# A four-part transformer block: the router splits nine weight pieces instead of 27, and the second attention's first batch is put in another order

## The reference, cut to what matters

```python
x = x + tanh(g_xattn[0]) * L0_xattn(layernorm(x), ctx, ctx, ...)   # 16 heads of 16, rotary positions
x = x + tanh(g_ffn[0])   * L0_ffn(layernorm(x), ...)               # 8 experts, top 2 of each token, and a shared expert
x = x + tanh(g_xattn[1]) * L1_xattn(layernorm(x), ctx, ctx, mask, ...)  # 16 heads of 64, masked softmax
x = x + tanh(g_ffn[1])   * L1_ffn(layernorm(x), ...)               # quantised gate/up/down

def L0_ffn(x):                                   # T = 4096 tokens
    scores = softmax(x @ gate_w.T);  _, indices = top_k(scores + gate_bias, 2)
    combine = sum_k one_hot(indices, 8) * take(scores, indices)
    y = sum_e mlp(x, w1[e], w2[e], w3[e]) * combine[:, e:e+1]
    return y + mlp(x, sw1, sw2, sw3)             # mlp: (silu(x @ w1.T) * (x @ w3.T)) @ w2.T, inner width 512
def L1_xattn(Q, K, V, mask):
    q, k, v = Q @ W_q + b_q, K @ W_k + b_k, V @ W_v + b_v         # inner width 1024
    s = where(mask == 0, -1e9, q k^T / 8);  return softmax(s) v @ W_o + b_o
```

## Time and profile before

| | |
|---|---|
| median of 3 runs | 2144.2 us (2143.4 to 2144.92) |
| the profiled execution | 2143.76 us, its span 2141.7 us |
| TensorE busy | 1743.6 us, 81% of the span |
| VectorE busy | 1415.4 us, 66% |
| ScalarE busy | 1103.9 us, 52% |
| GpSimd busy | 1034.0 us, 48% |
| granted TensorE clock, mean | 0.931 of full speed |

### The profile page before, as it was taken

How to read it: one execution, slowest core, us unless ns; L and a number is a source line. 1 busy time by engine, 2 the same in 40 slices (tenths; PEclk the granted TensorE clock), 3 DMA queues, 4 the chain that set the end, 5 groups by cost and what they waited for, 6 DMA issues and landing times. The chain is left out here.

```text
span 2141.7 us, 45574 instructions
## 1 busy us (share of the span) xinstructions
PE 1743.6 (81%) x14369; PEld 1163.1 (54%) x14375; DVE 1415.4 (66%) x2938; ACT 1103.9 (52%) x2568; POOL 1034.0 (48%) x1543
## 2 busy tenths in 40 slices
PE   0588888886258979999995899999999999998376
PEld 0344444443234546666663676767676767776123
DVE  4356667675975434444444787778787877877796
ACT  1266666664632212222221666666666666666776
POOL 1555555550735732232315666666666666554004
PEclk9689999998569999999997999999999999999697
DMA  3000000000820011222213222222232332320102
GB/s 104 12 9 12 10 10 10 10 5 1 267 78 1 1 47 57 69 71 63 79 44 94 70 73 70 69 72 69 74 78 69 78 77 70 79 63 11 41 1 79
DMA packets 89345, 117.62 MB, mean 55 GB/s; under 512 B 16520, under 2 KB 58768, under 8 KB 89232
## 3 DMA queue, kind: packets, MB, share of 16 engines
q1 hardware_dynamic: 76176, 90.08, 15.6%
q0 software_dynamic: 6528, 17.83, 3.0%
q10 hardware_dynamic: 6528, 8.39, 1.2%
HBM read 56.36 MB, written 17.83 MB: 35 GB/s over the span
## 5 line engine op out<-in xcount | busy, mean ns | idle before, releaser
L1069 POOL TENSOR_SCALAR a_P<-a_P,a_RS 128x256 f32<-128x256 f32 x512 | 254.5, 497 | 235.4 <-DVE a_RS L1351 206.1
L1238 ACT ACTIVATE a_P<-a_pS,a_NM 128x256 f32<-128x256 f32 x512 | 237.9, 471 | 198.3 <-DVE a_NM L1347 194.6
L815 DVE TENSOR_REDUCE a_M<-a_pS 128x2 f32<-128x512 f32 x256 | 164.6, 685 | 142.6 <-PE a_pS L626 142.3
L1247 ACT ACTIVATE a_PH<-a_pT 128x512 f16<-128x512 f32 x256 | 154.1, 602 | 80.5 <-PE a_pT L1163 70.5
L1347 DVE TENSOR_REDUCE a_NM<-a_pS 128x2 f32<-128x512 f32 x256 | 174.7, 682 | 26.3 <-PE a_pS L1155 20.7
L1357 DVE TENSOR_TENSOR a_PL<-a_pT,a_PH 128x512 f16<-128x512 f32 x256 | 172.5, 674 | 16.9 <-ACT a_PH L1247 16.8
L754 ACT ACTIVATE a_PT<-a_pT 128x512 f32<-128x512 f32 x256 | 139.0, 597 | 71.4 <-PE a_pT L645 71.1
L1163 PE MATMUL a_pT<-g_ident,a_P 128*128 128x128 f32 x1024 | 155.9, 275 | 19.9 <-POOL a_P L1069 19.9
L1163 PEld LDWEIGHTS a_pT<-g_ident,a_P 128*128 128x128 f32 x1024 | 120.0, 141 | 38.2 <-POOL a_P L1069 19.3
L1946 ACT ACTIVATE me_hh<-me_pH 128x512 f16<-128x512 f32 x72 | 43.0, 597 | 175.7 <-PE me_pH L1933 175.7
L99 PE MATMUL a_pF<-a_ch,xw_XW 128*128 128x256 f16 x512 | 103.1, 285 | 32.2 <-DVE a_VL L1339 29.2
(11 more groups left out here) (442 smaller groups left out, 5251.9 us busy)
## 6 DMA issues: line engine op xcount, KB each, us to landing
a_KD<-a_KN SPq DMA_DIRECT2D x128, 128.0 KB, 2.3
a_QS<-a_QN SPq DMA_DIRECT2D x128, 128.0 KB, 2.3
mr_stage<-mw SPq DMA_DIRECT2D x24, 512.0 KB, 4.7
ys<-me_yb SPq DMA_DIRECT2D x72, 128.0 KB, 1.7
a_ctxin<-ctxT SPq DMA_DIRECT2D x32, 256.0 KB, 2.7
a_KZ<-a_KN SPq DMA_DIRECT2D x64, 128.0 KB, 2.3
g_X<-x SPq DMA_DIRECT2D x1, 4096.0 KB, 15.1
rows<-mr_row ACTq DMA_DIRECT2D x32, 128.0 KB, 3.6
```

The costliest lines, as they stand in the source:

```text
L815: nc.vector.reduce_max(M[:, :, a, p2], pS[a][:], AX.X).then_inc(s_max.sem, 1)
L1069: last = nc.gpsimd.tensor_scalar(P32[u % 4][:, a, :], P32[u % 4][:, a, :], RS[u % 4][:, a:a + 1], LIFT, ALU.mult, ALU.mult)
L1238: last = nc.scalar.activation(P32[u % 4][:, a, :], pS[u % 2][:, a, :], ACT.Exp, bias=NM[u % 4][:, a:a + 1], accum_out=SM[u % 4][:, a:a + 1])
L1247: nc.scalar.activation(PH[p2 % 2][:, :, :, j * P:(j + 1) * P].rearrange("p a k q -> p (a k) q"), pT[u % 2][:].rearrange("p a k q -> p (a k ...
```

## The change

In `moe_router` only the first nine pieces (three experts: shared, 0 and 1) are split, and by GpSimd alone, conversion and subtraction in quarters of 256 columns. ScalarE normalises in VectorE's place, and SP issues the stores of the rows. The other 18 pieces are split in `moe_shared` as 36 halves: SP loads, ScalarE converts two per step from step 1, GpSimd subtracts. There the one-hot patterns are made by VectorE, four pairs by one instruction; the routing's parts get later steps and stand behind the low half; tables share buffers; the bias table is loaded in the router. In `attention1` comb(0)'s gathers and sums all run in turn 0, before front(0)'s pieces, and root and refinement in turn 1; VectorE clears KZ; the fold runs at turn 12 of front(0). In every batch x is normalised at turn 4 and transposed at turn 6, behind the keys; queries have turns 8 to 12 and values 13 to 17.

```diff
 # attention1
-    START = 2
-    HALF = [START + i * 2 // 3 for i in range(24)]
-    KEYS, QUERIES, VALUES = HALF[0:8], HALF[8:16], HALF[16:24]
+    KEYS, QUERIES, VALUES = ([start + i * 2 // 3 for i in range(8)] for start in (2, 8, 13))
+    NORMAL, TURNED = 4, 6
...
+    def at_once(p):
+        return plan(*[(0 if t < ROOT else 1, do) for t in sorted(p) for do in p[t]])
...
-        run(UNITS, comb(0, 0, 0))
-        run(UNITS, now(front(0, 0)), comb(1, 1, 0))
+        run(UNITS, at_once(comb(0, 0, 0)), now(front(0, 0)), beside, comb(1, 1, 0))
+        filled()
...
-            for z in (z for zs in KZ for z in zs):
-                nc.gpsimd.memset(z[64:P, :, :], 0.0).then_inc(cleared, 1)
-            pool.wait_ge(cleared, 5)
...
 # TensorE
                     xn_ready.wait(pe, b, 1)
-                    if not isinstance(b, int) or b:
-                        v_lo.wait(pe, b, -1)
+                    k_flat.wait(pe, b, 3)
...
                         if q == 0:
                             ctx_lo.wait(pe, b, 1)
+                            if not isinstance(b, int) or b:
+                                v_lo.wait(pe, b, -1)
+                        elif q == 1:
                             v_lo.wait(pe, b, 0)
-                        elif q == 1:
-                            x_lo.wait(pe, b, 1)
                         else:
                             k_flat.wait(pe, b, q - 1)
-                    chunk(1 + q, Wv["k"], ch[par], cl[par], q, a)
+                    chunk(q, Wv["k"], ch[par], cl[par], q, a)
...
-                        if q < 2:
-                            k_flat.wait(pe, b, 3 + q)
-                        else:
+                        if q == 0:
+                            k_flat.wait(pe, b, 4)
+                            x_lo.wait(pe, b, 1)
+                        elif q > 1:
                             q_lo.wait(pe, b, q - 1)
...
-                return plan((START, inputs), *[(KEYS[i], lambda i=i: keys(i // 2, i % 2)) for i in range(8)],
+                return plan(*[(KEYS[i], lambda i=i: keys(i // 2, i % 2)) for i in range(8)], (TURNED, inputs),
...
-            batches(pe, uncombined, front, back)
+            batches(pe, uncombined, front, back, plan((12, fold)))
...
 # VectorE
+            for z in (z for zs in KZ for z in zs):
+                nc.vector.memset(z[64:P, :, :], 0.0).then_inc(zeroed, 1)
...
-                return plan((0, normalised), (START, inputs), *[(KEYS[2 * q + 1], lambda q=q: keys(q)) for q in range(4)],
+                return plan((NORMAL, normalised), (TURNED + 1, inputs), *[(KEYS[2 * q + 1], lambda q=q: keys(q)) for q in range(4)],
 # moe_router
+            def load(j):
+                src, hi, lo = jobs[j]
                 if j >= NS:
-                    sp.wait_ge(w_lo, j - NS + 1)
+                    sp.wait_ge(w_lo, PIECES * (j - NS + 1))
...
+            for j in range(NS):
+                load(j)
+            for t in range(TILES):
+                store(t)
+                if t % 4 == 3 and NS + t // 4 < len(jobs):
+                    load(NS + t // 4)
...
         @block.gpsimd
-                pool.wait_ge(w_hi, j + 1)
-                nc.gpsimd.tensor_tensor(lo, stage[j % NS][:], hi, ALU.subtract).then_inc(w_lo, 1)
+                pool.wait_ge(staged[j % NS], 16 * (j // NS + 1))
+                for a in range(PIECES):
+                    cols = slice(a * PIECE, (a + 1) * PIECE)
+                    nc.gpsimd.tensor_copy(hi[:, cols], stage[j % NS][:, cols]).then_inc(w_hi, 1)
+                for a in range(PIECES):
+                    cols = slice(a * PIECE, (a + 1) * PIECE)
+                    pool.wait_ge(w_hi, PIECES * j + a + 1)
+                    nc.gpsimd.tensor_tensor(lo[:, cols], stage[j % NS][:, cols], hi[:, cols], ALU.subtract).then_inc(w_lo, 1)
...
         @block.scalar
+            def normalise(t):
+                if t > 1:
+                    lo_ready.wait(act, t, -1)
+                nc.scalar.activation(xn[t % 2][:], X[:, t, :], ACT.Identity, bias=nb[:, t:t + 1], scale=rstd[:, t:t + 1]).then_inc(xn_ready.sem, 1)
...
             for t in range(TILES):
-                store(t)
-                if t < len(jobs):
-                    weight_high(t)
                 if t + 2 < TILES:
+                    normalise(t + 2)
                     high(t + 2)
-                logits(t)
+                if t:
+                    logits(t - 1)
 # moe_shared
-    COUNT_AT, IDS_AT = 3, 10
+    COUNT_AT, IDS_AT = 4, 13
...
+            for n, (src, hi, lo) in enumerate(halves):
+                if n > 1:
+                    sp.wait_ge(w_lo, 2 * (n - 1))
+                sp.dma_start(stage[n % 2][:].rearrange("p (a b) -> p a b", a=src.shape[1]), src).then_inc(staged[n % 2], 16)
...
+            for n, (src, hi, lo) in enumerate(halves):
+                pool.wait_ge(w_hi, n + 1)
+                for cols in (slice(0, F0 // 2), slice(F0 // 2, F0)):
+                    nc.gpsimd.tensor_tensor(lo[:, cols], stage[n % 2][:, cols], hi[:, cols], ALU.subtract).then_inc(w_lo, 1)
...
             for g in range(STEPS):
                 silu(g)
+                if g and 2 * g - 2 < len(halves):
+                    weight_high(2 * g - 2)
                 high(g)
+                if g and 2 * g - 2 < len(halves):
+                    weight_high(2 * g - 1)
...
+            def patterns(n):
+                if n > 1:
+                    dve.wait_ge(hot_used, n - 1)
+                link(V.tensor_tensor(equal, ..., ALU.is_equal))
+                V.tensor_tensor(where[n % 2], ..., ALU.is_equal)
+                link(V.tensor_tensor(which[n % 2], equal, ..., ALU.mult))
+                dve.sem_inc(hot_ready, 1)
...
                 hidden(g)
-                routing(g)
                 if g >= FK and g % FK == 0:
                     for t in range(g - 4, g):
                         result(t)
                 low(g)
+                routing(g)
```

More of the change, by code:

```diff
@@ L953, in now, with batches @@
         return {t: p[t] for t in p if t < UNITS}
-    def batches(eng, comb, front, back):
+    def at_once(p):
+        return plan(*[(0 if t < ROOT else 1, do) for t in sorted(p) for do in p[t]])
+    def batches(eng, comb, front, back, beside={}, filled=none):
         def step(new, old, *soon):
@@ L1212, in inputs @@
                 def inputs():
-                    f_full.wait(act, b, 1)
+                    f_full.wait(act, b, 5)
                     nc.scalar.activation(xh[:].rearrange("p k t -> p (k t)"), pF[par][:], ACT.Copy).then_inc(x_hi.sem, 1)
@@ L1229, in values @@
                     nc.scalar.activation(VH[par][:, j, half * 512:half * 512 + 512], pF[(9 + n + par) % 2][:], ACT.Copy).then_inc(v_hi.sem, 1)
-                return plan((0, context_high), (START, inputs), *[(QUERIES[2 * q + 1], lambda q=q: queries(q)) for q in range(4)],
+                return plan((0, context_high), (TURNED + 1, inputs), *[(QUERIES[2 * q + 1], lambda q=q: queries(q)) for q in range(4)],
                             *[(VALUES[2 * q + 1], lambda q=q: values(q)) for q in range(4)])
@@ L1255, in back, with biases, fold @@
                         plan(*[(u, lambda u=u: exps(u)) for u in range(UNITS)]))
-            batches(act, uncombined, front, back)
+            batches(act, uncombined, front, back, plan((1, biases)))
         @block.vector
         def _(dve):
-            dve.wait_ge(consts_in, 64)
-            dve.wait_ge(folds, 2)
-            nc.vector.tensor_tensor(bvl[:], bvt[:], bvh[:], ALU.subtract).then_inc(folded, 1)
-            dve.wait_ge(folds, 3)
-            nc.vector.tensor_tensor(bo[:], bo[:], pG[:, 0:D], ALU.add).then_inc(folded, 1)
-            dve.wait_ge(folded, 2)
+            for z in (z for zs in KZ for z in zs):
+                nc.vector.memset(z[64:P, :, :], 0.0).then_inc(zeroed, 1)
+            def biases():
+                dve.wait_ge(consts_in, 64)
+                dve.wait_ge(folds, 2)
+                nc.vector.tensor_tensor(bvl[:], bvt[:], bvh[:], ALU.subtract).then_inc(folded, 1)
+            def fold():
+                dve.wait_ge(folds, 3)
+                nc.vector.tensor_tensor(bo[:], bo[:], pG[:, 0:D], ALU.add).then_inc(folded, 1)
+                dve.wait_ge(folded, 2)
             def comb(b, par, turn):
@@ L1305, in normalised @@
                     if not isinstance(b, int) or b:
-                        f_full.wait(dve, b, 1 - f_full.per)
+                        f_full.wait(dve, b, 5 - f_full.per)
                     for j in range(2):
@@ L1381, in back @@
                             *[(2 * p2 + LAG_PV, lambda p2=p2: out_low(p2)) for p2 in range(PAIRS)], (END, finish), (END + 1, statistics))
-            batches(dve, comb, front, back)
+            batches(dve, comb, front, back, plan((1, biases)), fold)
             measured.wait(dve, B, 0)
@@ L1535, in moe_shared @@
     scan = (bi, cand)
[L1536 to L1537 removed]
+    steps, more = s.sb("steps", [P, NE, TILES]), s.sb("more", [P, NE, TILES])
     tiles = s.sb("tiles", [P, NE])
```

(14 more changed lines are left out.)

205 lines of the change are left out of this document (114 added, 91 removed).

## The result

Forecast: 2103 us, between 2080 and 2127. Measured: the changed kernel 2098.6 us (median of 4, 2091.8 to 2099.0), the kernel before 2144.6 on the same chip, ratio 0.9772 with a 95% interval of 0.9749 to 0.9795. The profiled execution took 2099.0 us (span 2097.3). The forecast is 4.4 us off, but not because its terms were right.

| stage | before | after | change | forecast (ends) |
|---|---|---|---|---|
| router | 78.7 | 46.3 | -32.4 | -21 (-29, -12) |
| shared MLP | 160.7 | 181.7 | +21.0 | +10 (-6, +20) |
| routed MLP | 355.8 | 355.6 | -0.2 | 0 |
| first batch | 43.7 | 37.7 | -6.0 | -9 (-13, -5) |
| later batches | 802.5 | 770.5 | -32.0 | -21 (-30, -3) |

A forecast was written before the change was run, and what follows sets the result against it. Bounds by stage: VectorE, held by GpSimd, in the router; TensorE in shared MLP and later batches; a chain of waits in the first batch. Terms -21 + 10 - 9 - 21 = -41 from 2143.76 give 2103 us, range 2080 to 2127.

The forecast's parts named there:

- a piece costs 4 x 0.50 + 4 x 0.70 = 4.8 us: Router: GpSimd's four copies and four subtractions for one weight piece, with gaps between instructions; nine pieces 43 us.
- The hold: Router: VectorE's low half and GpSimd's instructions delay each other; 0.2 us lost by GpSimd per tile, 5.7 us a piece.
- Rival 1: Router and shared MLP: each low half waits out a quarter, each quarter a low half; router -12, MLP +14, 2116; chance 0.15.
- So 20.8 against 18.6: Shared MLP: four steps with weight halves take 20.8 us, including 1.7 for TensorE's lower clock, against 18.6 before.
- the ring: Shared MLP: weight halves pass through two stages, load, conversion, subtraction; a round takes 5.0 us and ScalarE waits for it.
- keeps its operations: Shared MLP: the routing, spread out at one choice a step behind the low half, keeps its operations.
- 19.6: Shared MLP: four steps with the one-hot patterns on VectorE, 3.75 us a step behind the down projection, take 19.6 us.
- if the MLP takes over 180 us: Shared MLP: one of the signs listed as showing the forecast wrong; the term itself was +10 us.
- Keys, zeroing: First batch: keys start 12 us earlier; VectorE's zeroing takes between nothing and 10 us, GpSimd's gathers come 7.0 us earlier.
- then the transposes: queries near 1150: First batch: after the keys' 7.7 us at the lower clock come x's transposes, so queries start near 1150 us.
- Behind it stand the maximum, the exponentials and, in ScalarE's queue, the last value conversion, so a_VL: Later batches: normalisation held at turn 0 delays a_VL; without it a_VL comes 1.6 us sooner; term -21 of 26.9.
- an end of the range: Later batches: the term's end of -30 us, with a lower clock that went with a stall now and then.

The follow-up runs named there:

- whole pieces: The changed kernel with the router's nine pieces converted and subtracted whole (1024 columns) instead of in quarters; 2101.0 us, ratio 0.979, router 51.2 us.
- identities later: The changed kernel with the shared MLP's identity matmuls one step later behind the patterns; 2091.1 us, ratio 0.974, shared MLP 180.5 us.
- x sooner in all batches: The changed kernel with x's high and low half at turn 6 instead of 7 in every batch; 2103.9 us, ratio 0.980, later batches 782.6 us.
- queries later: The changed kernel with the query chunks from turn 9 instead of 8 in every batch; 2096.1 us, ratio 0.977, later batches 768.6 us.

## Why the prediction was right, and where its steps were not

**The total** was right by luck, with terms that missed in opposite directions: 11 us too little gain in the router, 11 too little loss in the shared MLP, 3 too much gain in the first batch, 11 too little in the later ones. The four terms together came to -49.4 against -41, and 5 us of scatter in the untouched stages brought the spans' difference to -44.4. The parts below say which mechanisms held.

**Router.** Right: ScalarE takes the normalisation, GpSimd ends the stage. Mis-sized: "a piece costs 4 x 0.50 + 4 x 0.70 = 4.8 us", interpolated from the earlier trace rows. Left alone, GpSimd does four conversions and four subtractions in 3.9 us (the last three rows above: 549.59 - 545.71), 0.35 and 0.62 from one to the next; the conversion, drawn through the row of 32 columns (326 ns), is the larger miss. The hold took 0.6 from it, not the 0.9 I added: 4.5 a piece, 41 us for nine where I had 51. On VectorE the hold made 0.42 into 0.60 on the mean and 0.95 at the most, and it cost nothing, since VectorE had time. Rival 1 named the right mechanism: the hold is full, as whole pieces show. Its price was wrong, because a quarter's subtraction takes only 0.69 us. In two of eleven profiles there was a hold of another kind, that neither I nor the rival had, and there the router took 57.

**Shared MLP.** The step that failed is the one that carried the term: "So 20.8 against 18.6", all of it from the ring in ScalarE's order (the terms listed for it add up to 18.9 and not 19.1, and those of VectorE's chain to 19.5 and not 19.6, which changes little). ScalarE does wait for its stages' loads, as I said, but taking it out of the ring gave back only 5.3 us, 3 to 8 by the scatter of the stage. The routing "keeps its operations", I wrote, and costed their lengthening at nothing; it is 7 us. By step 12 the changed kernel was 9.3 us behind the kernel before where I had 3, by step 20 it was 17.4 where I had 8, and from there it lost 3.0 as against 2.5. VectorE's chain with patterns, "19.6", measures 20.1 without any weights beside it, since the operations take 1.9 us and not 1.6. What would show me wrong was "if the MLP takes over 180 us": it took 181.7, and that sentence did its work.

**First batch.** Keys, zeroing (0.91 each, 3.6 us in VectorE's idle time) and fold as costed. Failed: "then the transposes: queries near 1150". The low half of x stood behind the last keys' bias addition, itself 1.9 us late for GpSimd's split, and behind the next batch's combination. I had counted no queue on VectorE there. Putting it in front gave 34.4 us, near my figure. From there on it went as forecast: the first scores follow the last of the values at once, so TensorE itself ends last.

**Later batches.** "Behind it stand the maximum, the exponentials and, in ScalarE's queue, the last value conversion, so a_VL" is half of it, and the step that failed: the wait for a_VL went without the normalisation's move. The move took 0.8 us a batch off VectorE and 11 us of waits for a_ol off TensorE. Of the -32, the batches of 51.3 to 52.7 among 50.5 were 8 us, with a granted clock of 0.97 in three of the five; such batches are absent after, and the granted clock of the stage is 1.00 for 0.99. I had these only as an end of the range.

## What to carry to other kernels

An operation on VectorE that reads two SBUF tiles, and as the routing shows a tensor-scalar operation or a cast from SBUF to SBUF too, must be costed together with what GpSimd does at that moment, in every stage the edit reaches: moving GpSimd's work into a stage lengthens operations that the edit doesn't touch. A wait that an edit removes is a gain only if the engine it named isn't the pace: four times here (identities later, x sooner in all batches, queries later, and the keys in front of x's transposes with the normalisation at turn 0) the wait vanished and came back, whole or in the main, under another tile's name. Judge by the stage: a total that hits the expected figure can do so by the scatter of stages nobody changed.

## What was not expected of the hardware

A low half on VectorE, 0.42 us alone, took 12.40 us in one profile and 12.42 in another, of eleven with the same router. It began inside one quarter on GpSimd and ended only when GpSimd ran out of pieces: three pieces, some 24 instructions of 0.41 and 0.69 us, went past it. Beside it GpSimd ran at its undisturbed pace (3.9 us a piece), where in the other nine profiles the two took turns, at about 4.5. So the hold is not always over with the instruction that caused it; it cost the router 10 us (57.3 and 56.6 instead of 46.2 to 47.6). Both times the low half ended 0.3 us after the last of the run. What decides between the two was not tried; a gap in GpSimd's row, a DMA it waits for, ended it both times.
